# Moving 162 of 6400 attention score units from the ScalarE exponential to eight VectorE steps, on one core

## What is computed

```python
h = _L0_tok_ref(x, W, b, cls)                     # (4, 3137, 128)
# attention on layernorm(h)
attn = jnp.einsum('bhsd,bhtd->bhst', q, k) * scale + pos_bias
attn = jax.nn.softmax(attn, axis=-1)
out = jnp.einsum('bhst,bhtd->bhsd', attn, v)
h = h + out.transpose(0, 2, 1, 3).reshape(B, S, HIDDEN) @ Wo
# experts on layernorm(h): pooled over tokens, two of eight experts per image
h = h + _L0_ffn_ref(_layernorm(h), ...)
```

## Time and profile before

| | |
|---|---|
| median of 3 runs | 2861.55 us (2857.55 to 2865.6) |
| the profiled execution | 2861.5 us |
| its span on the core | 2859.8 us |
| instructions | 121986 |
| ACT busy | 2564.2 us, 90% of the span |
| PE busy | 2547.9 us, 89% |
| DVE busy | 846.0 us, 30% |
| POOL busy | 786.6 us, 28% |

### The profile page before, as it was taken

The page is one execution under the profiler, slowest core; times in us unless marked ns, Lnnn a source line. Parts: engine busy times, 40 slices in busy tenths (PEclk is TensorE's granted clock), DMA queues, the critical chain, the costliest instruction groups (busy, mean ns, idle before and its releaser), DMA issues.

```text
span 2859.8 us, 121986 instructions
## 1 busy us (share of the span) xinstructions
PE 2547.9 (89%) x55860; PEld 1222.0 (43%) x55860; DVE 846.0 (30%) x1246; ACT 2564.2 (90%) x2733; POOL 786.6 (28%) x1424
## 2 busy tenths in 40 slices
PE   7988888888889999888899898889999988999997
PEld 3443333333344444433444444334444433455554
DVE  4760111111114233311243343112433421244410
ACT  4769999999999999999999999999999999744553
POOL 2112333333333333333333333332333333100000
PEclk8989999999999999999999999999999999999998
DMA  5550001111111100011111000101110000300010
GB/s 129 176 174 7 29 30 32 32 32 32 33 42 35 35 30 30 30 47 33 42 36 35 30 30 29 49 32 40 35 35 29 29 29 31 127 26 29 15 35 19
DMA packets 65897, 125.31 MB, mean 44 GB/s; under 512 B 10034, under 2 KB 55180, under 8 KB 63892
## 3 DMA queue, kind: packets, MB, share of 16 engines
q1 hardware_dynamic: 63324, 110.93, 12.2%
q0 software_dynamic: 2048, 6.43, 0.6%
HBM read 67.30 MB, written 51.30 MB: 41 GB/s over the span
## 4 chain that ended last, share of the span: by engine, by line
ACT 51%; PE 26%; issue 19%; DMA 2%; DVE 1%; POOL 0%; SPq 0%; ACTq 0%; POOLq 0%
ACT shared L846 50%; PE ps L714 6%; PE ps L722 6%; PE ps L750 5%; PE ps L671 3%; PE ps L668 2%; PE ps L698 1%; DMA k_halves<-halves 1%; PE ps L612 1%; PE ps L606 1%; PE ps L627 0%; DMA band_rows<-band_sb 0%; DVE std L968 0%; POOL ln L915 0%; PE ps L620 0%
## 5 line engine op out<-in xcount | busy, mean ns | idle before, releaser
L846 ACT ACTIVATE shared<-ps 128x1179 f32<-128x1179 f32 x2167 | 2246.4, 1302 | 5.9 <-PE ps L671 4.3
L750 PE MATMUL ps<-shared,va 64*32 64x393 f32 x25600 | 1573.1, 499 | 1.1 <-issue 0.8
L929 POOL TENSOR_TENSOR shared<-shared,e_all 128x310 f32<-128x310 f32 (+19 forms) x1344 | 728.5, 554 | 1539.5 <-ACT shared L846 1533.0
L671 PE MATMUL ps<-qa,ka 48*32 48x393 f16 (+2 forms) x15200 | 728.1, 319 | 149.9 <-ACT shared L846 149.0
L668 PE MATMUL ps<-qa,ka 51*32 51x393 f16 (+8 forms) x13184 | 655.9, 314 | 104.3 <-ACT shared L846 103.8
L750 PEld LDWEIGHTS ps<-shared,va 64*32 64x32 f32 x25600 | 620.3, 139 | 28.9 <-issue 4.5
L671 PEld LDWEIGHTS ps<-qa,ka 48*32 48x32 f16 x15200 | 229.8, 90 | 630.9 <-ACT shared L846 619.7
L668 PEld LDWEIGHTS ps<-qa,ka 51*32 51x32 f16 x13184 | 205.8, 89 | 660.6 <-ACT shared L846 658.7
L1006 DVE COPY xc<-ps 128x393 f32<-128x393 f32 x64 | 36.4, 568 | 1102.6 <-PE ps L750 1102.5
L865 ACT ACTIVATE qa<-ps,b 128x393 f32<-128x393 f32 x256 | 136.4, 585 | 85.0 <-PE ps L714 84.9
L1014 DVE RECIPROCAL sq<-sq 128x393 f32<-128x393 f32 x64 | 167.3, 2615 | 2.2
(11 more groups left out here) (143 smaller groups left out, 1320.7 us busy)
## 6 DMA issues: line engine op xcount, KB each, us to landing
qa<-q_halves SPq DMA_DIRECT2D x64, 196.5 KB
ka<-k_halves SPq DMA_DIRECT2D x64, 196.5 KB
att_rows<-std SPq DMA_DIRECT2D x64, 196.5 KB, 3.4
v_rows<-v_sb SPq DMA_DIRECT2D x4, 1600.0 KB, 6.9
va<-v_rows SPq DMA_DIRECT2D x32, 200.0 KB, 15.9
ln_rows<-ln SPq DMA_DIRECT2D x32, 196.5 KB, 5.6
q_halves<-halves SPq DMA_DIRECT2D x32, 196.5 KB, 3.1
k_halves<-halves SPq DMA_DIRECT2D x32, 196.5 KB, 4.2
```

The costliest lines, as they stand in the source:

```text
L671: last = nc.tensor.matmul(out[x:y, cut:W], ka[r:r + 48, par, k0 + x:k0 + y], qa[r:r + 48, par, q0 + cut:q0 + W], start=True, stop=True, ti ...
L750: last = nc.tensor.matmul(ps[quad:quad + 32, O_PS + half, 0:W], va[r:r + 64, par, :, kt], pr[r:r + 64, g % SLOTS_PR, j], start=(kt == 0), ...
L846: nc.scalar.activation(pr[:, g % SLOTS_PR, 0:m], ps[:, b0:b0 + m, 0:W], ACT.Exp, scale=1.0 / (LIFT * LIFT)).then_inc(s_exp, 1)
L929: nc.gpsimd.tensor_tensor(p, p, e_all[0:keys, n % HEADS, t:t + z - a], ALU.mult).then_inc(s_biased, 1)
```

## The change

1. A group in `d_at` (162 of them) still holds three units, but its ACTIVATE takes the first two. The third unit's exponential is made by DVE, in eight instructions: two read the bank, then PE may write it again (`s_d_read`), six more work in SBUF on the tile `root`.
2. These units lie 18 apart in passes that have no guests (wanted positions 28, 46, 64, 82), and 20 apart in the others (33, 53). The first unit from there on whose third unit lies off the band is taken.
3. Guests move to positions 30, 50 and 70 of passes 1 to 13, with V always at 70; before they were at 35, 58 and 80 of passes 1 to 11.
4. The values of a batch with such a unit come seven groups later instead of four, and later batches of the pass may go ahead of it.
5. The scores are scaled by -log2(e) for DVE's steps, and the result of both paths carries the factor exp(0.386), which the softmax takes out again. For this, ACT's exponential has a new scale and a bias that it reads from a tile, `lift_t`.
6. On SP's queue one load of a guest's input moves one head later, and the maximum, sum and pick of the gate move with the guests.

```diff
+LIFT = 64.0
+LOG2E = 1.4426950408889634
+EXP_LIFT = 0.386022442659754
+ROUND = LIFT * LIFT * (1.5 * 2.0 ** 23 + 197)
+D_LAG = 7
+GUEST_POS = (30, 50, 70)
...
+    busy = {q // PASS for q in places} | {2 * HEADS * (b + 1) + p for b in range(B - 1) for p in (13, 14, 15)}
+    wanted = [q * PASS + pos for q in range(1, 2 * NBH) for pos in ((33, 53) if q in busy else (28, 46, 64, 82))]
...
+        elif len(d_at) < len(wanted) and u >= wanted[len(d_at)] and u + 2 < len(units) and plain(u + 2):
+            d_at[len(groups)] = len(d_at)
...
@@ SP
                     if b >= 0 and into == 2:
                         load_attention(b, 6)
+                    if b >= 0 and into == 3:
                         load_attention(b, 7)
@@ PE, scores
+                    if g - AHEAD in d_at:
+                        pe.wait_ge(s_d_read, d_at[g - AHEAD] + 1)
@@ PE, values
+                    for u in batches[m]:
+                        if u in d_unit:
+                            pe.wait_ge(s_d_exp, d_unit[u] + 1)
@@ ACT
+                act.wait_ge(s_lift, 1)
                 for g in range(NG):
...
-                    m = len(groups[g])
+                    m = len(groups[g]) - (g in d_at)
                     b0 = GMAX * (g % 2)
                     nc.scalar.activation(pr[:, g % SLOTS_PR, 0:m], ps[:, b0:b0 + m, 0:W],
-                                         ACT.Exp, scale=1.0 / (LIFT * LIFT)).then_inc(s_exp, 1)
+                                         ACT.Exp, bias=lift_t[:, 0:1], scale=-1.0 / (LOG2E * LIFT * LIFT)).then_inc(s_exp, 1)
@@ DVE
+                nc.vector.memset(lift_t[:], EXP_LIFT).then_inc(s_lift, 1)
...
+                def exponential(k):
+
+                    g = d_group[k]
+                    score = ps[:, GMAX * (g % 2) + 2, 0:W]
+                    x, whole, p = root[:, 0], root[:, 1], root[:, 2]
+                    if k > 0:
+                        dve.wait_ge(s_d_exp, k)
+                    dve.wait_ge(s_score, g + 1)
+                    nc.vector.tensor_scalar(whole, score, ROUND, None, ALU.add).then_inc(s_d_step, 1)
+                    dve.wait_ge(s_d_step, k * D_STEPS + 1)
+                    nc.vector.scalar_tensor_tensor(x, whole, ROUND, score, ALU.subtract, ALU.subtract).then_inc(s_d_read, 1)
+                    dve.wait_ge(s_d_read, k + 1)
+                    nc.vector.scalar_tensor_tensor(p, x, EXP2[4], x, ALU.add, ALU.mult).then_inc(s_d_step, 1)
+                    nc.vector.tensor_scalar(whole.bitcast(I32), whole.bitcast(I32), 23, EXP_BITS,
+                                            ALU.logical_shift_left, ALU.bitwise_xor).then_inc(s_d_step, 1)
+                    for i in range(3):
+                        dve.wait_ge(s_d_step, k * D_STEPS + 3 + i)
+                        nc.vector.scalar_tensor_tensor(p, p, EXP2[3 - i], x, ALU.add, ALU.mult).then_inc(s_d_step, 1)
+                    dve.wait_ge(s_d_step, k * D_STEPS + 6)
+                    if g >= SLOTS_PR:
+                        dve.wait_ge(s_pv, BATCHES + batches_until(g - SLOTS_PR))
+                    nc.vector.scalar_tensor_tensor(pr[:, g % SLOTS_PR, 2], p, EXP2[0], whole, ALU.add, ALU.mult).then_inc(s_d_exp, 1)
...
                 for g in range(NG + 4):
+                    if g in d_at:
+                        exponential(d_at[g])
                     if g in guest_at:
                         receive(guest_at[g], GMAX * (g % 2) + 2)
```

More of the change, by code:

```diff
@@ L81, in score_groups, with guest_plan @@
     return groups + tail
-def guest_order():
-    steps = []
-    for s in range(CH + 3):
-        for kind, lag in (("Y", 0), ("M", 1), ("V", 2), ("S", 3)):
-            if 0 <= s - lag < CH:
-                steps.append((kind, s - lag))
-    return steps + [("G", 0)]
+def guest_plan():
+    seen = {"Y": 0, "M": 0, "V": 0, "S": 0}
+    plan = []
+    for p in range(1, 2 * HEADS):
+        y_here = False
+        for pos in GUEST_POS:
+            if pos == GUEST_POS[2]:
+                kinds = [("V", "M")]
+            else:
+                kinds = [("S", "V"), ("M", "Y"), ("Y", None)]
+            for kind, after in kinds:
+                c = seen[kind]
+                if c < CH and (after is None or c < seen[after]) and not (kind == "Y" and y_here):
+                    seen[kind] += 1
+                    y_here = y_here or kind == "Y"
+                    plan.append((kind, c, p, pos))
+                    break
+    assert len(plan) == 4 * CH and plan[-1][2] <= 13
+    return plan + [("G", 0, 15, GUEST_POS[0])]
 def fast_order(B, KT):
@@ L98, in fast_order, with plain @@
     units = [(n, kt, 4 * side + c) for n in range(NBH) for side in range(2) for kt in range(KT) for c in range(4)]
-    places = []
-    for b in range(B - 1):
-        q = 2 * HEADS * (b + 1)
-        places += [(q + 1 + i // 3) * PASS + (35, 58, 80)[i % 3] for i in range(4 * CH)] + [(q + 14) * PASS + 58]
-    groups, guest_at, u = [], {}, 0
+    plan = guest_plan()
+    places = [(2 * HEADS * (b + 1) + p) * PASS + pos for b in range(B - 1) for kind, c, p, pos in plan]
+    busy = {q // PASS for q in places} | {2 * HEADS * (b + 1) + p for b in range(B - 1) for p in (13, 14, 15)}
+    wanted = [q * PASS + pos for q in range(1, 2 * NBH) for pos in ((33, 53) if q in busy else (28, 46, 64, 82))]
+    def plain(u):
+        n, kt, c = units[u]
+        lo = kt * P - REACH
+        return kt < KT - 1 and max(lo, c * (-(-((KT - 1) * P + 65) // CH)), 0) >= min(lo + BAND, (c + 1) * (-(-((KT - 1) * P + 65) // CH)))
+    groups, guest_at, d_at, u = [], {}, {}, 0
     while u < len(units):
@@ L112, in fast_order @@
     batches = [list(range(m, m + 4)) for m in range(0, len(units), 4)]
-    return units, groups, batches, guest_at
+    return units, groups, batches, guest_at, d_at
 def build(nc, B, S, d):
@@ L373, in build @@
             GUESTS = 4 * CH + 1
+            D_STEPS = 6
             EW = 16 * 8
@@ L398, in build @@
             DELAY = 2
-            units, groups, batches, guest_at = fast_order(B, KT)
+            units, groups, batches, guest_at, d_at = fast_order(B, KT)
+            assert T == (KT - 1) * P + 65
             NG = len(groups)
@@ L754, in values @@
                     last.then_inc(s_pv, 1)
-                done = 0
-                for g in range(NG + DELAY + AHEAD):
+                for g in range(len(turns)):
                     if g < NG:
                         scores(g)
-                    turn = 1
                     if g in guest_at:
                         visit(guest_at[g], GMAX * (g % 2) + 2)
-                        turn = 0
-                    while done < NB:
-                        lag = g - group_of[batches[done][-1]] - (done % KT == 0)
-                        if lag < DELAY + AHEAD or (turn == 0 and lag < HOLD):
-                            break
-                        values(done)
-                        done += 1
-                        turn = 0
-                while done < NB:
-                    values(done)
-                    done += 1
+                    for m in turns[g]:
+                        values(m)
                 pe.wait_ge(s_exp, NG)
```

44 lines of the change are left out of this document (36 added, 8 removed).

## The result

The changed kernel takes 3043.03 us (median of 4 runs, 3039.49 to 3047.63), the kernel before, now over 4 runs, 2862.03 us (2857.55 to 2865.6): a ratio of 1.0645 on record, with an interval of 1.0627 to 1.0662 (the two medians alone give 1.0632). It is 181 us slower. The forecast was 3012 us, 151 us slower, with a range up to 3045. The median of 3043 is 2 us inside that range; the 1.0645 on the 2861.55 us shown above are 3046, just outside. So the sign and the main term came true, and some 31 us were missed. The profiled execution took 3047.63 us, 1.7 more than its span.

The account below looks back on a forecast made before the run. ACT's exponential was taken to bound attention. 2861.5 - 53 (units off ACT) + 195 (bias read) - 11 (waits behind guests) + 20 (DVE's lateness) = 3012 us; range 2985 to 3045.

Parts of the forecast that it names:

- the main term: ACT's exponentials in attention: reading the bias from a tile adds 0.09 us to each of 2167, 195 us more.
- The bias read: Each of ACT's 2167 exponentials reads its bias from a tile, 0.09 us more, not hidden by a long predecessor; 195 us.
- Rival 1: ACT's exponentials: the bias read is hidden behind the long instruction before it, 0 instead of 195 us; 2848 us, chance 0.12.
- Rivals 2 and 3: Attention: bias read half hidden, 2920 us, chance 0.04; or POOL and DVE pile up, 3092 us, chance 0.04.
- rival 3: Some 80 DVE chains on the band take 7.6 us, over the 6.5 spacing; ACT stands about 1 us each; chance 0.04.
- 162 units: Attention: 162 units leave ACT at 0.33 us each, 53 us less.
- Waits behind guests: Attention: ACT's 99 waits of 0.11 us for scores behind a guest go, 11 us less.
- DVE's lateness: Passes with guests: DVE's steps come late and hold up PE and then ACT, some 20 us; none at least, 40 at most.
- the three patterns: Late chains: guest V behind a pushed chain, 8 us; guest at 51 between chains, 5; chain directly behind guest M, 6.
- Work hidden at no cost: Put at nothing: memset of `lift_t`, guests' new places, reordered values, chunk 7's load on SP's queue, the gate's moves.
- The signs given for the profile after: Ends 1.14 and 0.81 us apart, ACT idle about 20 us, DVE busy about 1600 us, counts 162 and 99 + 162.

Follow-up runs that it names:

- e1: The kernel before, with only the bias of its 2167 exponentials read from a tile of zeros; 3044.08 us, ratio 1.0639.
- e4: The changed kernel with the bias as an immediate and the old order of guests for the last image; 2843.62 us, ratio 0.9940.
- e2: The changed kernel with the same bias given as an immediate number instead of from a tile; 2870.33 us, ratio 1.0043.
- e9: e4 with DVE's exponentials only in the passes without guests, 72 instead of 162; 2838.25 us, ratio 0.9921.
- e6: e3 with guests at 35, 58 and 80 and DVE's exponentials at 41 and 62 in passes with guests; 3002.13 us, ratio 1.0508.
- e7: e4 with no exponential on DVE and one more wait for the last guest S before the pooling maximum; 2861.73 us, ratio 1.0013.
- e3: The changed kernel with the old order of guests for the last image alone; 3019.98 us, ratio 1.0564.
- e10: e6 with a group's first unit's scores computed twice in 527 groups, away from guests and DVE's exponentials; 2995.14 us, ratio 1.0472.
- e8: e3 with the first unit's scores computed twice in every second group without a guest or DVE exponential (954 groups); 3019.75 us, ratio 1.0566.

## Why the prediction was wrong, point by point

- **The bias read, 195 us.** Right in mechanism and size: 0.088 us instead of 0.09 for each instruction, 191 us, and e1 shows it alone (2861.5 + 191 = 3052 by the profile, 3050.57 in its profiled run). The reading of the earlier trace rows held, that a long predecessor hides nothing. Rival 1 would have been 2848 us; with the tile's price taken away and the late order repaired (e4) it is 2843.6. Rivals 2 and 3 are out: the ends are 1.13 apart, and the 162 chains lasted 4.97 us in the mean and 6.05 at the most, where rival 3 needed 7.6.
  The Trainium skill, page "ScalarE: Activation LUTs", section "What ACT_TABLE_LOAD costs", has about 93 ns for such an operand; e1 and e2 agree in size with 88 ns, and they add that it isn't hidden.
- **162 units, 53 us.** Right: e9 has 23.5 us for 72, 0.326 each. Both terms together, the pace, are +138 us against 142.
- **Waits behind guests, -11 us.** Right: the groups directly behind a guest stood out by 11.8 us before and by 0.0 in e1.
- **DVE's lateness, +20 us.** Right, a little high: the three patterns stand where they were named, 13.3 us of PE's waits, and 14 to 18 us come back in e6. At ACT's quick pace they cost 35 (e9 against e4), where rival 1 had 39.
- **"Work hidden at no cost: ... the guests' new places (same count of two-unit groups, 99)."** This is the step that failed, by 23 us. It counted two-unit groups and did not look at the second use of the same list: the order of the guests in the fourth image, where no attention lies between V and S. The move cost almost nothing in attention (3.7 us, e7) and 23 to 27 in the experts' stage (e3, e4). The others (the memset, chunk 7's load, the gate's moves) weren't tested one by one; e7 keeps them and puts them together with the guests' places at 3.7 us. The reordered values, also put at nothing there, are not in e7, since it holds no batch back: no run prices them, and the trace has 18 of the 23 half-clock places behind pauses in the values, which the reordering made 134 of 47.
- **A term that wasn't in the sum: the granted clock.** The forecast said that PE would wait longer for ACT and took that for free. PE's clock fell to half in 23 places, 14 of them with the slower pace alone (e1). With the places where it coincides with other stalls, the excess of attention is +28 us instead of +9: lateness 14, -9 for what goes outside such places with the slower pace (e1), and about 23 that go with half-clock places, of which 8 to 17 are the clock's by e10 and the bare places. Some 6 to 15 us of excess stay without a cause that a run isolates: they stand in the same places, beside guests and chains. The earlier trace rows showed 1066 pauses of PE for ACT on one line, 0.57 us in the mean (after 966 of 0.65), and the prediction didn't ask what longer ones do. The Trainium skill, page "TensorE: Matmul & The Clock Gate", section "A second HAM failure mode: psum-queue depth-cycling", describes a TensorE that idles briefly between groups of matmuls while it cycles through banks, so that its clock swings between half and full. The trace agrees in kind: 23 falls to half, with pauses of 0.62 us in each turn ahead of the one shown.
- **The signs given for the profile after.** Ends of 1.14 and 0.81 (1.134 and 0.808), DVE busy about 1600 us (1618.8), 162 + 99: right. ACT's idle time of 20 us was 35. Attention +150 was +166. The whole: 3012 + 23 (late order) + 15 (attention) - 2.7 (the start) = 3047, the profiled run, which stands 4.6 us over the median.

The range was too narrow for one reason: it varied only the terms in the sum, and both misses were edits or effects set to zero.

## What to carry to other kernels

An operand from SBUF for the bias costs an ACTIVATE 0.088 us here even when the value is constant and the instruction long; with thousands of them on the path, give a constant as an immediate. When a table that orders work is rewritten, follow every stage that reads it, the last image's or the last tile's too: there the distance between a producer and its consumer may shrink from 20 groups to one unit. Work handed to an engine with much idle time pays in full, within the spread of the runs, where its chains stand alone (0.326 us for each unit in e9) and not at all where they stand right ahead of work that another engine waits for; the places are worth as much as the number.

## What the runs showed of the hardware

TensorE's granted clock can cost time in a kernel that waits for ACT and not for PE. Between 300 and 2400 us its mean was 0.98 with 23 places at 1.2 GHz in all of attention where PE was busy for 1841 us (after and e3), and 1.00 with 3 and 4 places where it was 1867 and 1874 us (before and e8). The total doesn't decide it (26 places with 1855 us in e6, 5 with 1858 in e2): ahead of 18 of the 23 places PE made no values for 2.3 us or more, and each turn of its wait for ACT was longer than before (0.62 us instead of 0.53 in the rows shown). A place takes an estimated 0.4 to 0.84 us from ACT. Extra scores took 19 of the places away in e8 and brought no time, since they made other scores late, behind two-unit exponentials above all.
